# Three moves in the state-space stage: the tanh of even convolution tiles in its bank, the skip products behind the exponential, the gated tile's high and low part in its own step

## What is computed

```python
proj = jnp.einsum('bld,pd->blp', hidden_states, in_proj_w)      # gate, x/B/C, dt
conv = conv_bias
for k in range(K):                                              # K = 4 taps
    conv = conv + pad[:, k:k + L, :] * conv_weight[:, k]
xBC = jax.nn.silu(conv)                                         # x: 64 heads of 64; B, C: 8 groups of 128
dt_p = jax.nn.softplus(dt + dt_bias); dA = jnp.exp(dt_p * A); dtx = dt_p[..., None] * x
def step(state, inp):
    state = state * dA_t[..., None, None] + dtx_t[..., None] * B_t[:, :, None, :]
    y_t = jnp.einsum('bhpn,bhn->bhp', state, C_t)
y = jnp.moveaxis(ys, 0, 1) + x * D[None, None, :, None]          # the skip products
yn = (yg * lax.rsqrt(var + EPS)).reshape(B, L, I) * norm_weight  # by group of 512
yn = yn * jax.nn.silu(gate)                                      # the gated tile
out = jnp.einsum('bli,di->bld', yn, out_proj_w)
```

## Time and profile before

| | |
|---|---|
| median of three runs | 1784.63 us (1781.35 to 1789.15) |
| the profiled execution | 1799.58 us, of which the span of instructions is 1797.8 us |
| PE busy | 1571.5 us (87%) |
| DVE busy | 1229.0 us (68%) |
| POOL busy | 942.2 us (52%) |
| ACT busy | 828.4 us (46%) |
| mean granted clock of TensorE | 0.938 |
| state-space steps | from 94 to about 1046 us |
| chain that ended last | PE 61%, DVE 16%, POOL 8%, issue 7%, ACT 4% |

### The profile page before, as it was taken

One profiled execution on the slowest core, in us unless ns is written; L12 is line 12 of the kernel. 1 busy time (PEld: TensorE's weight loads), 2 busy tenths in 40 slices (PEclk: granted clock), 3 DMA queues, 4 the chain that ended last, 5 costly groups with the idle time before them and its releaser, 6 DMA issues.

```text
span 1797.8 us, 26599 instructions
## 1 busy us (share of the span) xinstructions
PE 1571.5 (87%) x8870; PEld 1235.1 (69%) x8870; DVE 1229.0 (68%) x2024; ACT 828.4 (46%) x1639; POOL 942.2 (52%) x861
## 2 busy tenths in 40 slices
PE   3789999999989999999999759995689999988791
PEld 2567877877878777778787547884456776766581
DVE  5577777778778777787787765556547766768525
ACT  2355554544544544555544323332047666664131
POOL 3257567576566675765766643004334423427454
PEclk9899999999999999999999879998789999998796
DMA  3102011011021110110211012231000000041334
GB/s 113 36 15 87 19 48 59 12 47 60 15 70 37 44 58 18 47 60 14 83 31 46 14 59 73 69 114 36 0 1 13 13 1 1 1 165 71 110 137 164
DMA packets 49497, 92.60 MB, mean 52 GB/s; under 512 B 8016, under 2 KB 32720, under 8 KB 44176
## 3 DMA queue, kind: packets, MB, share of 16 engines
q1 hardware_dynamic: 45744, 79.58, 13.8%
q0 software_dynamic: 3680, 12.06, 2.0%
HBM read 81.14 MB, written 10.49 MB: 51 GB/s over the span
## 4 chain that ended last, share of the span: by engine, by line
PE 61%; DVE 16%; POOL 8%; issue 7%; ACT 4%; DMA 3%; SPq 1%; another core or an unknown queue 0%; POOLq 0%; ACTq 0%; DVEq 0%
PE banks L355 30%; PE banks L1717 6%; PE banks L1836 3%; PE banks L1641 3%; PE banks L1635 3%; PE banks L1727 2%; PE banks L1795 2%; POOL wol L360 2%; DMA x<-in_w_gate 2%; DVE tap L1195 2%; PE banks L1826 2%; PE banks L1650 2%; DVE xbc L1201 2%; DVE acc L623 2%; PE banks L1609 2%
## 5 line engine op out<-in xcount | busy, mean ns | idle before, releaser
L1195 DVE SCALAR_TENSOR_TENSOR tap<-banks,parg,tap 128x511 f32<-128x511 f32 (+2 forms) x288 | 215.1, 747 | 41.3 <-ACT tap L922 33.9
L705 POOL TENSOR_TENSOR am<-ah,upto 128x1024 fp32r<-128x1024 f32 x64 | 124.3, 1942 | 216.3 <-PE banks L1609 201.3
L857 POOL TENSOR_SCALAR kz<-kst,head 128x512 fp32r<-128x512 f32 x64 | 99.1, 1567 | 160.2 <-DVE kst L1413 160.2
L355 PE MATMUL banks<-xTh,wch 128*128 128x512 f32 x384 | 163.5, 426 | 8.1 <-DVE em L1299 7.8
L355 PE MATMUL banks<-xTh,wcl 128*128 128x512 f32 x384 | 151.3, 394 | 0.0
L355 PE MATMUL banks<-xTl,wch 128*128 128x512 f32 x384 | 151.1, 393 | 0.0
L1127 ACT ACTIVATE prob<-banks,nmax 128x128 f32<-128x128 f32 (+3 forms) x256 | 121.8, 530 | 53.9 <-DVE nmax L1429 53.8
L930 ACT ACTIVATE th<-tap 128x512 f32<-128x512 f32 x96 | 60.6, 631 | 171.2 <-DVE tap L1195 169.1
L1429 DVE TENSOR_REDUCE nmax<-banks 128x2 f32<-128x256 f32 (+3 forms) x128 | 104.9, 819 | 39.9 <-PE banks L1827 39.7
L705 POOL TENSOR_TENSOR am<-al,upto 128x1024 fp32r<-128x1024 f32 x64 | 123.7, 1932 | 0.0
L922 ACT ACTIVATE tap<-banks,parg 128x512 f32<-128x512 f32 x96 | 74.6, 777 | 92.3 <-PE banks L355 91.2
(11 more groups left out here) (289 smaller groups left out, 4492.5 us busy)
## 6 DMA issues: line engine op xcount, KB each, us to landing
x<-grownT SPq DMA_DIRECT2D x96, 128.0 KB, 4.8
x<-in_w_conv SPq DMA_DIRECT2D x7, 1536.0 KB, 6.7
x<-in_w_gate SPq DMA_DIRECT2D x8, 1024.0 KB, 5.1
x<-in_w_out SPq DMA_DIRECT2D x8, 1024.0 KB, 4.8
eraw<-in_expert_w SPq DMA_DIRECT2D x8, 1024.0 KB, 7.2
gur<-in_ff_gu SPq DMA_DIRECT2D x7, 1024.0 KB, 4.8
x<-in_hidden SPq DMA_DIRECT2D x16, 256.0 KB, 4.1
mates<-yd SPq DMA_DIRECT2D x8, 512.0 KB, 4.3
```

The costliest lines, as they stand in the source:

```text
L355: m = nc.tensor.matmul(o, a, b, start=first and n == 0, stop=last and n == len(terms) - 1)
L705: m = pool.tensor_tensor(am[:, part, :, :], a[:, i, :].bitcast(F32).unsqueeze(2).to_broadcast([P, HG, P]), upto[:, :].unsqueeze(1).to_broa ...
L857: m = pool.tensor_scalar(kz[:, quad % 2, p2, j, :], kst[:, p2, :].bitcast(F32), head[:, j:j + 1], None, ALU.mult)
L1195: nc.vector.scalar_tensor_tensor(tap[:, q % 2, sh:L], bk(CONV_BANKS[q % 2])[:, 0:L - sh], parg[:, KC * q + k:KC * q + k + 1], tap[:, q % 2 ...
```

## The change

Three things move.

1. The tanh of an even tile is written into bank 0, over the convolution's own sums, and not into `th`; `silu` reads it there. `th` is left to the odd tiles. What comes next into bank 0, the gate tile, so waits for `xbc_ready` of tile 0 (the `silu`) where it waited for `taps`; in the prologue the even tiles wait in the same way.
2. The skip products `xd` are made in the step that adds them, behind the exponential and ahead of the first tap, not at the end of the step before. The copy of `skipg` goes to the end of step 0, with a semaphore.
3. The high part `ynTh` is made at the end of the step that makes the gated tile, behind the second tanh, and the low part `ynTl` behind the second `silu`. The gated product itself is moved on DVE from behind tile 1's taps to ahead of tile 0's `silu`. ACT's wait for the output product is kept, one chunk on: there is one `ynTh`.

The core of the diff:

```diff
+        def kept_tanh(q):
+            return th[:, :] if q % 2 else bk(CONV_BANKS[0])
...
             def tanh(n, q):
                 act.wait_ge(taps, 3 * n + 3)
-                if not (isinstance(n, int) and n < 1):
-                    act.wait_ge(xbc_ready, n)
-                nc.scalar.activation(th[:, :], tap[:, q % 2, :], ACT.Tanh).then_inc(tanh_ready, 1)
+                if q % 2:
+                    at_least(act, xbc_ready, n - 1)
+                nc.scalar.activation(kept_tanh(q), tap[:, q % 2, :], ACT.Tanh).then_inc(tanh_ready, 1)
...
-                if not (first and s < 2):
-                    act.wait_ge(yn_ready, NT * g + i + 1)
-                    at_least(act, o_ready, NT * g + i)
-                    nc.scalar.copy(ynTh[:, :, :], kt(bk(6))).then_inc(ynT_hi, 1)
...
+                if not (first and s == 0) and s <= NT:
+                    at_least(act, y_ready, NT * g + s - 1)
+                    if s == 1:
+                        act.wait_ge(cur_ready, 2 * g + 2)
+                    j = (s - 1) % NT
+                    for k in range(KT):
+                        n = nc.scalar.activation(xd[:, k, :], xbc[:, k, j * P:(j + 1) * P], ACT.Copy, scale=skipg[:, k:k + 1])
+                    n.then_inc(xd_ready, 1)
...
-                if s < NT:
-                    if not (first and s == 0):
-                        act.wait_ge(y_ready, NT * g + s)
-                    for k in range(KT):
-                        n = nc.scalar.activation(xd[:, k, :], xbc[:, k, s * P:(s + 1) * P], ACT.Copy, scale=skipg[:, k:k + 1])
-                    n.then_inc(xd_ready, 1)
+                if not (first and s == 0) and s <= NT:
+                    act.wait_ge(yn_ready, NT * g + s)
+                    at_least(act, o_ready, NT * g + s - 1)
+                    nc.scalar.copy(ynTh[:, :, :], kt(bk(6))).then_inc(ynT_hi, 1)
...
-                nc.vector.scalar_tensor_tensor(xbc[:, q, b * L:(b + 1) * L], th[:, :], 1.0,
+                nc.vector.scalar_tensor_tensor(xbc[:, q, b * L:(b + 1) * L], kept_tanh(q), 1.0,
...
-                if not (first and s < 2):
-
-                    dve.wait_ge(ynT_hi, NT * g + s - 1)
-                    low(nc.vector, ynTl[:, :, :], kt(bk(6)), ynTh[:, :, :]).then_inc(ynT_lo, 1)
...
+                if making:
+
+                    dve.wait_ge(ynT_hi, NT * g + i + 1)
+                    low(nc.vector, ynTl[:, :, :], kt(bk(6)), ynTh[:, :, :]).then_inc(ynT_lo, 1)
...
                     if tiles:
-                        pe.wait_ge(taps, 3 * (n0 + tiles[0]) + 3)
+                        pe.wait_ge(xbc_ready, n0 + tiles[0] + 1)
                     else:
                         pe.wait_ge(gate_used, NT * g + s + 3)
                     gated(*gate, 0)
...
                 pe.wait_ge(taps, 3 * (q - 1))
+                if q % 2 == 0:
+                    pe.wait_ge(xbc_ready, q - 1)
                 convolved(q, q, 0)
```

More of the change, by code:

```diff
@@ L743, in step @@
                 if s == 0:
-                    pool.wait_ge(cur_ready, g + 1)
+                    pool.wait_ge(cur_ready, 2 * g + 1)
                 if s < NT:
@@ L1304, in step @@
                     convolve(n0 + tiles[0], tiles[0] % CT)
-                if s == 0:
-                    nc.vector.tensor_copy(skipg[:, :], skip[:, bass.ds(g, 1), :].rearrange("p g k -> p (g k)"))
                 if making:
@@ L1323, in step @@
                             nc.vector.tensor_tensor(state[:, :], bk(6), state[:, :], ALU.add).then_inc(state_ready, 1)
+                if making:
+                    dve.wait_ge(gate_used, NT * g + 4 + KT * (i // CH) if i >= 0 else NT * g)
+                    if c < CH - 1:
+                        dve.wait_ge(state_ready, m + c + 1)
+                    dve.wait_ge(sq_ready, NT * g + i + 1)
+                    nc.vector.tensor_tensor(kt(bk(6)), kt(bk(7)), gate_at(i % NT), ALU.mult).then_inc(yn_ready, 1)
                 if s == 3 and not last:
@@ L1329, in step @@
                     convolve(n0 + tiles[1], tiles[1] % CT)
-                if making:
-                    dve.wait_ge(gate_used, NT * g + 4 + KT * (i // CH) if i >= 0 else NT * g)
-                    if c < CH - 1:
-                        dve.wait_ge(state_ready, m + c + 1)
-                    dve.wait_ge(sq_ready, NT * g + i + 1)
-                    nc.vector.tensor_tensor(kt(bk(6)), kt(bk(7)), gate_at(i % NT), ALU.mult).then_inc(yn_ready, 1)
                 if gate:
@@ L1341, in step @@
                     silu(n0 + tiles[1], tiles[1] % CT, tiles[1] // CT % NB)
+                if s == 0:
+                    nc.vector.tensor_copy(skipg[:, :], skip[:, bass.ds(g, 1), :].rearrange("p g k -> p (g k)")).then_inc(cur_ready, 1)
+                if making:
+                    dve.wait_ge(ynT_hi, NT * g + i + 1)
+                    low(nc.vector, ynTl[:, :, :], kt(bk(6)), ynTh[:, :, :]).then_inc(ynT_lo, 1)
                 i = s - 2
```

## The result

| | before | changed |
|---|---|---|
| median | 1786.89 us (1781.35 to 1793.55, 4 runs) | 1928.67 us (1926.63 to 1929.61, 4 runs) |
| ratio | | 1.0805 (95% interval 1.0772 to 1.0839) |
| profiled execution | 1799.58 us | 1929.61 us |
| mean granted clock | 0.938 | 0.922 |

The changed kernel is 8% slower: 142 us by the medians, 130 by the two profiled executions. Forecast were 1926.6 us, with a range of 1873 to 1986.

A forecast was written before the change was run, and what follows sets the result against it. TensorE's issue was taken to bound the state-space stage. From the runs' median of 1784.6 us, 129 for stalls and 66 for clock falls, less 53 gained, gave 1926.6 us, range 1873 to 1986.

The forecast's parts named there:

- What bounds the kernel: State-space stage: TensorE's issue bounds it, PE busy 898.94 of 952.00 us, so PE waits in most steps add one for one.
- The stalls, 129 us: PE waits before the gate for tile 0's silu: 36 steps lose 2.83 us, 8 lose 3.44, 129 us in all.
- The clock, 66 us: PE's clock falls after the 44 stalls, 1.5 us each: 66 us, bounds 0 and 123.
- The gain, 53 us: Earlier high and low parts and moved skip products remove PE waits in the stage: 53 us saved, 45 to 63.
- Step 3: Step 3 over eight groups: PE no longer waits for ynTl or the xtok copy, saving 34.5 us of the gain.
- Step 5: Step 5 over the groups: 6.9 us idle and 1.6 of clock in group 0 disappear, 8.5 us of the gain.
- Step 7: Step 7: PE's 0.58 us wait for ynTl goes in each of seven groups, 4 us of the gain.
- The last group: Steps 4 to 7 of the last group, without tiles: 6 us of the gain from 15.2 idle, bounds 0 and 15.
- The clock holds: Rival: stalls in the state-space stage bring no clock fall, so 1860.6 us; chance 0.11.
- long falls: Rival: each of the 44 stalls costs a long clock fall of 2.8 us, 123 in all, so 1984 us; chance 0.10.
- gain missing: Rival: the low part still comes late for step 3 and PE idles as before, so 1980 us; chance 0.06.
- Hidden wait: Rival: the gate's wait on the silu costs PE next to nothing and 53 us are gained, so 1732; chance 0.02.

The follow-up runs named there:

- filled stalls: The changed kernel with 11 unused matmuls of 512 columns added between tile 1 and the gate in every stalling step: 1874.93 us, ratio 1.0499.
- without the bank: The changed kernel with every tile's tanh in SBUF again and the gate waiting for the taps, gated product still ahead: 1751.05 us, ratio 0.9815.
- second profile: The kernel before, unchanged, profiled once more: 1788.94 us, its eight steps 3 summing to 111.20 us.
- earlier trace: The first profile of the kernel before, unchanged, from which the prediction was read: 1799.58 us, its eight steps 3 summing to 122.19 us.
- the order taken back: The changed kernel with the gated product behind tile 1's taps again, the tanh still in its bank: 1808.9 us, ratio 1.0134.
- the Square first: The changed kernel with ACT's Square moved ahead of tile 1's first tap: 1880.37 us, ratio 1.0511.
- five matmuls: The changed kernel with 5 unused matmuls of 512 columns added in each stall: 1886.36 us, ratio 1.0508, measured on another chip.

## Why the prediction came true, point by point

- **What bounds the kernel.** Held. Step 1 of group 3, at the full clock, idled 2.78 us and was 3.05 longer than before, and where the clock fell as well the step was longer by the idle time and the fall. DVE's busy time fell by 16 us and nothing came of it, as in the row of its costliest kinds: the `silu` took a mean of 1017 ns before, and these are its two forms now:

```profile
L1207 DVE SCALAR_TENSOR_TENSOR xbc<-th,tap 128x512 f32<-128x512 f32 x48 | 32.9, 684 | 0.0
L1207 DVE SCALAR_TENSOR_TENSOR xbc<-banks,tap 128x512 f32<-128x512 f32 x48 | 32.7, 681 | 0.7 <-ACT banks L934 0.7
```

- **The stalls, 129 us.** Right in kind and size: 124 us between the kernel with filled stalls and the one without the bank, and 130.2 us in the row of waits. The single stall was 2.93 where I had 2.83 in the ordinary steps; step 4 had 3.05 of idle time before the gate where I had 2.67; step 2 had 3.33 (some 3.3 forecast).
- **The clock, 66 us.** Right in kind, a fifth too large: 54, or 1.2 us per stall, where I took 1.5 from rows with shorter stalls in two pieces. It also isn't the same for each stall: 34 of 44 paid about 1.6, ten nothing. My sign for it was wrong: I wrote that the clock would show 0.8 to 0.9 over the stage, and it showed 0.94. 66 us of loss in some 1090 make 0.94 as well, so this was an error of arithmetic against my own term.
- **The gain, 53 us.** Right in kind, and the term that was most mis-sized: 34.5 us by the medians of the kernel without the bank (33 by its ratio). The profile of the kernel without the bank, beside the second profile of the kernel before, gives what each term of it was worth. *Step 3*, 34.5 in the sum: 20.7 (111.2 less 90.5 for the eight). The 122.19 of the earlier trace rows was read from a profile in which step 3 was of the slow kind in four groups, 11.0 us of it, and step 3 doesn't reach 10.84 without the stalls: in group 3 it lasts 11.29, where the changed kernel has 10.41. *Step 5*, 8.5: nothing, the seven last 114.0, where they lasted 113.6 (114.87 in the earlier trace rows). *Step 7*, 4: 5.2. *The last group*, 6: 15.8, as these two rows show, its steps from 4 on up to the last output product, in the kernel before (second profile) and without the bank:

```profile
981.12:1050.29 69.17, 48.67 (x259) 37.81 (x257) 47.36 (x89) 18.88 (x42) 43.38 (x48) 0.85 0.13 43
958.79:1012.13 53.34, 43.93 (x259) 34.46 (x257) 44.80 (x89) 19.89 (x46) 42.27 (x47) 0.94 0.18 55
```

And the sum had no term for what is lost: step 4 is longer by 2.4 us in seven groups, step 6 by 2.1. So the term of step 3 and that of step 5 were too large by 23 us together, and the last group, which the forecast held to 0 to 15 us, gave back 10.
- **The sum.** 124 + 54 - 34.5 = 143.5 against a measured 142 and a forecast of 142. These three are differences along one row of kernels, so that they close by themselves and don't confirm each other; where the stalls end and the gain begins depends on the row. The three terms were off by -5, -12 and +18.5 us. That they cancel to 2 us is luck. The range doesn't rest on it: had the three errors added up, to 36 us, the result would still lie inside. Setting the sum against the profile gave 1941.6, 12 us off; setting it against the median of the runs hid that the gain was read from the slow profile.
- **The rivals.** "The clock holds" is refuted by the filled stalls, "long falls" by 1.2 us per stall (four of the 44 did cost 2.7 to 2.9), "gain missing" by step 3 without a wait. "Hidden wait" had its condition named rightly: with the product behind, step 1 idles only 0.05 us. But the other steps keep 0.8 to 2.5, so the time would not have been 1732; with the order taken back it is 1808.9.
- **The signs.** The gate's matmuls have 135.0 us of idle time before them, 130.2 by DVE xbc, more than the 100 to 120 that I wrote and in keeping with the sum's own 129; steps with a stall last 17.1 to 22.4 (17.5 to 20), since the longest falls came in steps that were long already; step 3 lasts 10.41 (11).

## What to carry to other kernels

When a result is kept in a matmul's bank, the bank is held until its last reader has run, and the wait of the next matmul into it moves down the whole chain to that reader: follow that chain over every engine's order, and look for a link that itself waits for the matmul just issued. Two edits can be far dearer together than apart (here 52 us for the bank, 6 us gained by the moved product, 171 lost by both), so a bundle of them should be timed as a square. And a term that is read from one profile needs a second profile, where two engines become ready within a few hundredths of a microsecond.

## What the runs showed of the chip

- Single stalls of PE of up to 1.7 us never brought its clock from 2.4 to 1.2 GHz in the kernels with the Square first and with five matmuls; of those of 1.8 to 2.2 us 6 of 16 did, of those of 2.7 to 3.4 us 34 of 44, most of them for 1.3 to 1.6 us beyond the stall. Stalls of one length fell in some steps and not in others. Unused matmuls in the stalls gave 54 us back.
- Two instructions ready within 0.02 us of each other on DVE and POOL, both reading SBUF: either DVE's took 2.42 us and POOL's 1.90, or DVE's 0.68 and POOL's 2.45, and this moved a whole execution by some 10 us.
- The `silu` with one input in the bank took 0.68 us in each of the 46 cases of the changed kernel in which POOL was at work beside it; with both in SBUF, in the kernel before, 21 of 42 took longer than 0.8 us.
